# Level 0 of the blockwise inverses on TensorE: four 32x32 tiles with 16 columns to a pair of heads, in place of two 64x64 tiles with 32 columns

## The reference

```
S = a_t[..., None] * S
kp = einsum('bhd,bhde->bhe', kn, S)
S = S + b_t[..., None, None] * kn[..., None] * (v_t - kp)[..., None, :]
o = einsum('bhji,bhj->bhi', S, q_t)
R = aR_t[..., None] * R
kpR = einsum('bhd,bhde->bhe', kn, R)
R = R + g_t[..., None, None] * kn[..., None] * (r - kpR)[..., None, :]
o = o + einsum('bhji,bhj->bhi', R, q_t)
```

## Time and profile before

| | |
|---|---|
| median of 3 executions | 2249.17 us (2247.22 to 2252.94) |
| the profiled execution: its own time | 2257.42 us |
| its span, first to last instruction | 2255.3 us |
| TensorE matmul busy | 2189.8 us, 97% |
| TensorE weight load busy | 1835.1 us, 81% |
| VectorE, ScalarE, GpSimd busy | 76%, 46%, 51% |
| mean granted TensorE clock | 0.979 |

### The profile page before, as it was taken

The page is one execution under the profiler, slowest core; times in us unless marked ns, Lnnn a source line. Parts: engine busy times, 40 slices in busy tenths (PEclk is TensorE's granted clock), DMA queues, the critical chain, the costliest instruction groups (busy, mean ns, idle before and its releaser), DMA issues.

```text
span 2255.3 us, 114185 instructions
## 1 busy us (share of the span) xinstructions
PE 2189.8 (97%) x49472; PEld 1835.1 (81%) x49472; DVE 1717.1 (76%) x3728; ACT 1045.4 (46%) x2137; POOL 1145.6 (51%) x2384
## 2 busy tenths in 40 slices
PE   8999987899999999999999999999999999999998
PEld 3455545689888888888888888888888888888987
DVE  5501115688888888888888888888888888898864
ACT  3333245355545555555555555544445555555520
POOL 0010004556666666666666666666666666666541
PEclk9999999799999999999999999999999999999987
DMA  3000000222232222222332223222322233333331
GB/s 95 0 1 0 22 0 17 69 68 68 69 80 64 63 66 63 68 68 68 76 72 69 67 68 71 67 66 67 79 65 68 68 71 73 73 73 73 73 72 29
DMA packets 336175, 134.90 MB, mean 60 GB/s; under 512 B 285504, under 2 KB 324544, under 8 KB 335680
## 3 DMA queue, kind: packets, MB, share of 16 engines
q1 hardware_dynamic: 334480, 125.24, 23.5%
q10 hardware_dynamic: 1200, 2.36, 0.3%
HBM read 66.69 MB, written 60.82 MB: 57 GB/s over the span
## 4 chain that ended last, share of the span: by engine, by line
PE 94%; DVE 1%; DMA 1%; issue 1%; POOL 1%; ACT 1%; SPq 0%; POOLq 0%; DVEq 0%; ACTq 0%
PE bank L571 13%; PE bank L596 5%; PE bank L587 5%; PE bank L419 4%; PE bank L432 4%; PE bank L617 3%; PE bank L608 3%; PE bank L641 3%; PE bank L673 3%; PE bank L661 3%; PE bank L732 3%; PE bank L537 3%; PE bank L518 3%; PE bank L505 3%; PE bank L528 3%; PE bank L548 3%
## 5 line engine op out<-in xcount | busy, mean ns | idle before, releaser
L1207 POOL TENSOR_TENSOR lane_t<-lane_n,lane_x 128x15 f32<-128x15 f32 (+7 forms) x960 | 305.6, 318 | 339.4 <-DMA lane_n<-n_dram 269.2
L571 PE MATMUL bank<-kq,Kt 64*64 64x96 f32 x8192 | 358.0, 232 | 5.3 <-DVE AS L978 4.3
L1210 POOL TENSOR_TENSOR lane_x<-lane_x,lane_t 128x15 f32<-128x15 f32 (+7 forms) x960 | 292.2, 304 | 75.2
L571 PEld LDWEIGHTS bank<-kq,Kt 64*64 64x64 f32 x8192 | 311.7, 135 | 9.3 <-issue 8.9
L1164 POOL TENSOR_TENSOR dk<-cum 128x512 f32<-128x512 f32 x64 | 69.7, 1088 | 276.4 <-DVE cum L927 276.4
L1401 ACT ACTIVATE kend<-Kt,ek 128x64 f32<-128x64 f32 x768 | 189.5, 336 | 0.0
L1357 ACT ACTIVATE dk<-ea,small 128x512 f32<-128x512 f32 x128 | 92.4, 722 | 202.6 <-DVE ea L913 109.1
L1181 POOL TENSOR_TENSOR KQF<-efull,kn 128x768 f32<-128x768 f32 x64 | 133.6, 2087 | 82.4 <-ACT efull L1379 82.3
L927 DVE TENSOR_TENSOR_SCAN cum<-rst,dk 128x512 f32<-128x512 f32 x128 | 155.4, 1214 | 2.4 <-ACT dk L1357 2.4
L978 DVE COPY_PREDICATED AS<-cst,bank 128x384 f32<-128x384 int32 x256 | 141.2, 576 | 9.1 <-PE bank L571 9.0
L869 DVE TENSOR_TENSOR dn<-bank,s3b 128x512 f32<-128x512 f32 x8 | 5.5, 691 | 172.1 <-PE bank L444 168.0
(11 more groups left out here) (163 smaller groups left out, 5979.5 us busy)
## 6 DMA issues: line engine op xcount, KB each, us to landing
k_dram<-kend SPq DMA_DIRECT2D x64, 384.0 KB, 3.1
kend_in<-k_dram SPq DMA_DIRECT2D x256, 96.0 KB, 2.4
XF<-x_dram SPq DMA_DIRECT2D x256, 64.0 KB, 2.4
lane_n<-n_dram SPq DMA_DIRECT2D x128, 124.0 KB, 3.2
x_dram<-lane_x SPq DMA_DIRECT2D x128, 124.0 KB, 2.4
n_dram<-AS SPq DMA_DIRECT2D x256, 32.0 KB, 2.0
n_dram<-AR SPq DMA_DIRECT2D x256, 32.0 KB, 1.6
wt<-in_win SPq DMA_DIRECT2D x4, 640.0 KB, 4.6
```

Source lines behind the costliest of these rows:

```text
L571: ins = pe.matmul(v3(dst[hd[h], o:o + kinds * C], kinds)[:, :, i * SUB:(i + 1) * SUB], Kt[hd[h], m * 96 + i * SUB:m * 96 + i * SUB + C], r ...
L1207: pool.tensor_tensor(tv, lane_n[:, m * SUB + m + 1:m * SUB + BASE].unsqueeze(2).to_broadcast([L, rows, m + 1]), xv[:, m, 0:m + 1].unsqueez ...
L1210: pool.tensor_tensor(xv[:, m + 1:, 0:m + 1], xv[:, m + 1:, 0:m + 1], tv, ALU.subtract).then_inc(s["lane_step"], 1)
```

## The change

Both level-0 functions go from 64x64 to 32x32 tiles. Instead of one call for each head (64 rows, 64 stationary columns, 32 moving columns), there is one for each 32-partition quadrant e = 0 to 3, which holds one diagonal 32x32 block: 32 rows, 32 stationary columns, 16 moving columns. Calls go from 32 to 64 in each of the two functions, passes from 64 to 128. Only the half of IV that the masked copy takes is now written; the other 16 columns of each quadrant keep what was there, and they are read by ScalarE's copy as before, and dropped by the mask. No wait, no semaphore, no DMA and no other engine's instruction changes.

```diff
@@ level0_nx
-                            for h in range(2):
-                                ins = pe.matmul(IV[hd[h], m * SUB:(m + 1) * SUB], prod(n, y, c, p, 0)[hd[h], :],
-                                                v4(XF[hd[h], :], NM, 2)[:, m, :, 0:BASE], start=True, stop=True)
+                            for e in range(4):
+                                quad, i = slice(e * SUB, (e + 1) * SUB), e % 2
+                                ins = pe.matmul(IV[quad, m * SUB + i * BASE:m * SUB + (i + 1) * BASE], prod(n, y, c, p, 0)[quad, i * SUB:(i + 1) * SUB],
+                                                XF[quad, m * C + i * SUB:m * C + i * SUB + BASE], start=True, stop=True)
@@ level0_zd
-                    for h in range(2):
-                        ins = pe.matmul(IV[hd[h], m * SUB:(m + 1) * SUB], P0[hd[h], m * C:(m + 1) * C],
-                                        v4(Zf[n % 2][hd[h], :], NM, 2)[:, m, :, BASE:], start=True, stop=True)
+                    for e in range(4):
+                        quad, i = slice(e * SUB, (e + 1) * SUB), e % 2
+                        o = m * C + i * SUB
+                        ins = pe.matmul(IV[quad, m * SUB + i * BASE:m * SUB + (i + 1) * BASE], P0[quad, o:o + SUB],
+                                        Zf[n % 2][quad, o + BASE:o + SUB], start=True, stop=True)
```

## The result

The changed kernel takes 2571.5 us (median of 4; 2564.25 to 2587.21) against 2251.1 (2247.22 to 2257.01): 1.142 times as long, 95% interval 1.138 to 1.146. The forecast was 2281, range 2222 to 2342. The sign was right, the size ten times too small. The profiled execution took 2564.25 us, its span 2562.1. Executions over 1.5% above the fastest of their kernel (one of e1's, one of e9's, four of e14's) are left out of the medians and ratios further down.

What follows compares the result with a forecast made beforehand. TensorE's order was taken as the bound: 1.2 us a period saved, 1.7 us of new instruction-packet pauses, net +0.5 us, times 64 is 32 us; 2257.4 becomes 2289 profiled, 2281 as median, range 2222 to 2342.

Steps and rivals of the forecast that it cites:

- Four tiles at once: Level-0 functions L587 and L596: four 32x32 tiles run side by side, so each takes 1.13 us against 1.84.
- the 0.12 for leaving the tiles: Behind each level-0 function: going from 32x32 tiles back to other shapes costs 0.12 us.
- Rival 2: Level 0: the array takes passes no faster than in level 1; +1.4 us a period, +88 us, 2337; chance 0.13.
- Moving columns don't set the pace: Level-0 passes: stationary columns set the time, so 16 moving columns in place of 32 give nothing.
- 64 packets more, pauses 256 instructions apart in and behind the level-0 functions: TensorE's stream: some 64 more instruction packets; "issue" pauses at L587, L596, L608, L617 sum to 1.5 to 2 us a period.
- I take their mean, 3.14 us, as what a packet needs: TensorE's instruction supply: a packet of 256 instructions takes at least 3.14 us, bounds 2.86 and 3.37.
- The three rows: Stretch from L608 on, before the change: 256 instructions with a TensorE pause took 2.86, 3.20 and 3.37 us.
- the densest place: From L608 into L617: 250 seen instructions hold 2.6 us without a pause, and TensorE did pause there.
- placing (b): Packet boundary in the middle of L587: pauses of 0.65, 0.4, 0.2 and 0.4, in all 1.65 us a period.
- other traffic at that place: Stated way to be wrong: other traffic there, not what the three rows say, sets a packet's least duration.
- rival 4: Stretch in small tiles: the clock falls to 1.2 GHz, costing hundreds of microseconds; chance 0.02.
- VectorE's lateness: VectorE comes late by 0.5 us, all but some 0.1 covered ahead of L608; gain at most about 1.05 us a period.

Runs made afterwards that it cites:

- e1: Changed kernel with only the first level-0 function in 32x32 tiles, the second as before; 2427.5 us, 1.078 times the kernel before.
- e9: Kernel before plus one TensorE wait ahead of L587 on VectorE's clipping of chunk 2, a 1.2 us pause each period; 2457.0 us, ratio 1.087.
- e14: e7 with SyncE's kend transfer to DRAM sent ahead of the n_dram transfers; 2270.6 us, 1.012 times the kernel before.
- e3: Changed kernel with each 32x32 call moving up to 64 columns instead of 16; 2459.1 us, 1.093 times the kernel before.
- e7: Kernel before with ten already met TensorE waits a period left out, making six whole packets; 2229.9 us, ratio 0.992.
- e8: e7 plus 390 met waits at TensorE's start, so a packet begins at the head of level 1; 2278.2 us, 1.013 times the kernel before.
- e11: e10 plus 284 met waits at TensorE's start to shift the packet boundaries; 2585.2 us, 1.145 times the kernel before.
- e13: e11 with SyncE's kend transfer to DRAM sent ahead of the n_dram transfers; 2582.7 us, 1.150 times the kernel before.
- e6: Kernel before plus one TensorE wait ahead of L587 on VectorE's k operands, a 2.35 us pause each period; 2601.5 us, ratio 1.156.
- e5: Changed kernel with state R's half of level 0 left out of both functions; 2240.8 us, 0.996 times the kernel before.
- e10: Changed kernel with ten met TensorE waits a period left out, making seven whole packets; 2594.5 us, 1.148 times the kernel before.
- e4: Changed kernel with each call over all 64 rows of a head and 32 stationary columns; 2537.2 us, 1.130 times the kernel before.

## Why the prediction was right and wrong

**Four tiles at once: right.** 128 passes in 1.19 us (1.13 was forecast), and 0.38 for L689 behind it against 0.26 before, the 0.12 for leaving the tiles. The loss of the array's share is nil: at full clock and less its pauses a period takes 27.3 us, forecast 27.2. Rival 2 is out.

**Moving columns don't set the pace: right from 16 to 32.** 128 passes of 16 columns in four tiles take 1.19 us, 64 of 32 columns in two (L608) 1.13. With 64 columns (e3) a function takes 1.86 us, so there they do.

**64 packets more, pauses 256 instructions apart in and behind the level-0 functions: right.** That a late packet makes the pauses is shown by e7 and e8, where the place of the boundaries alone moves 2.2%.

**"I take their mean, 3.14 us, as what a packet needs": wrong.** This is the first step that failed. A packet that ends with a pause of over 0.15 us lasts 3.9 us in the median after (90% under 5.4, at most 6.8). The three rows were three packets whose fetch began 0.3 to 0.7 us after their first instruction. The trace of before had more to say: between 450 and 2150 us it has some 30 packets that end with such a pause right behind a fetch, and they last 2.8 to 7.2 us, 3.6 in the median. The prediction took its three from the densest place, where a packet can be short, and its upper bound of 3.37 is below that median. (In its side sums, placing (b) comes to 0.48 at 2.8 us a packet and to 2.6 at 3.37, rather than 0.35 and 2.5; neither moves the result by more than 0.1 us a period.) In the changed kernel's pauses of over 1.5 us the fetch begins mostly 0.8 to 3.5 us after that instruction, 1.8 in the median, by which time 240 of the packet's 256 instructions have started (median). What holds from one kernel to the next is the rest: about 1.0 us for the fetch and 1.4 until TensorE goes on. As a term of the sum the pauses measured 3.0 us a period against 1.9: 64 x 1.1 = 70 us of the miss. The prediction itself named the danger (other traffic at that place); by e11 and e13 the traffic is a part of it, and the late request the larger.

**The clock, rival 4: wrong, and the larger part.** I gave it 0.02 because level 1's small tiles ran at full clock. That was evidence on tiles and said nothing on pauses. The sum took pauses of 1.9 us a period and never asked what they do to the clock. TensorE hardly ever paused before, but the trace has two waits of over 1 us in attention's last units, ahead of L708 at 2157.81 and ahead of L587 at 2216.32 (waits, then windows of the kernel before):

```profile
PE bank L708 <- DVE yR L1059: 1.5, 1, 1.5
PE bank L587 <- DMA XF<-x_dram: 2.1, 2, 1.4
...
2160.10:2180.50 20.40, 20.01 (x399) 19.30 (x397) 10.68 (x26) 1.19 (x2) 8.48 (x31) 0.50 0.23 66
2218.10:2238.50 20.40, 19.59 (x407) 18.67 (x405) 7.87 (x23) 1.79 (x3) 0.00 (x0) 0.50 0.04 11
```

Behind each the clock is at half for over 20 us, with TensorE busy; the last digits of the clock in the earlier trace rows, 8 and 7, come from there. Two cases prove no cause, but they speak against a chance of 0.02 for a fall of the clock. e6 shows that pauses do it without a small tile; e9 that 1.2 us once a period is enough. What isn't shown is that the small tiles have no part in it: beside pauses, e3's wider passes leave a quarter of the time at the lower clock. After, 8.2 us of each period run at 1.2 GHz, which costs 3.3 us, 0.4 us for each (in e6 the 7.36 us cost 34.37 less its shortest period, 30.94: 3.4, or 0.47 for each): 64 x 3.3 = 211 us.

2289 (the sum for the profiled execution) + 70 + 211 = 2570; it took 2564. The 3.3 is what was left of the period, so that the sum closes is no proof of its parts; e6 is.

**VectorE's lateness: not tested.** With pauses TensorE never got so far ahead, as the prediction said; e5's chain suggests instead that the lanes of GpSimd come next.

**What stays open.** What the request for a packet hangs on, and so where a dense stretch should lie. How much of the time at the lower clock the small tiles add to what the pauses do. e11's placing was worked out from a wrong duration; others weren't tried. How e14's earlier transfer costs 2% isn't settled either: its profiled execution took only 2251.3 us, the least of ten. That a pause of 1.2 us (e9) has 4.5 us at the lower clock behind it and one of 2.35 us (e6) 7.4 is a result, not a mechanism.

## What to carry to other kernels

A faster form of a TensorE stage that doubles its instructions has to be priced in instructions per time: here, in the changed kernel, 73 of 77 packets with under 3 us of work ended with a pause, 21 of 40 with 3 to 4, and 7 of 239 with more. The packets' places in the stream alone were worth 2.2% before the change; after it two placings (e10, e11) took the same time. Then price each new pause twice, once for itself and once for the clock behind it, which here cost as much again; an engine that hardly pauses in the profile before says little on the second, and its few pauses have to be looked up one by one. A stretch that repeats is best made a whole number of packets long with the dense part clear of a boundary, which gave 0.8% here for ten waits left out.

## What the runs showed of the hardware

Tiles that share rows but not columns also run side by side: 128 passes of 64x32 tiles took 1.27 us (e4), against 1.84 for 64 of 64x64. The lower clock came with pauses of 1.2 and 2.35 us that recur once a period (clock 0.93 in e9, 0.90 in e6), and for 20 us behind single ones of 1.5 and 1.4 us (before). It doesn't slow all passes alike: L537 goes from 1.06 to 2.00 us, L620 from 1.13 to 1.84. An instruction packet's fetch can start after all instructions of the packet ahead of it have started (1658.16 against 1657.35). The Trainium skill (Runtime: NRT & Kernel Launch, Instruction fetch mechanics) says that the next page is fetched "while executing the current one"; that wasn't so there, and the traces agree with the hiding that it describes only where the stream is slow, as in e7, where no packet takes less than 3.9 us and none comes late.
